# Second attention layer: scores from two fp32r parts, two sides of 64 rows each in the array

## What is computed

```python
q = _apply_rotary((x @ Wq.T).reshape(B, T, H, Dh), cos, sin)
k = _apply_rotary((x @ Wk.T).reshape(B, T, H, Dh), cos, sin)
v = (x @ Wv.T).reshape(B, T, H, Dh)
scores = jnp.einsum('bhqd,bhkd->bhqk', q, k) * scale
scores = jnp.where(causal[None, None], -jnp.inf, scores)
attn = jax.nn.softmax(scores, axis=-1)
out = jnp.einsum('bhqk,bhkd->bhqd', attn, v)
x = x + out.transpose(0, 2, 1, 3).reshape(B, T, C) @ Wo.T
```

## Time and profile before

| | us |
|---|---|
| median of 3 runs | 2464.02 |
| lowest, highest | 2453.02, 2469.33 |
| the profiled execution | 2465.51 |
| its span, first to last instruction | 2463.4 |
| PE busy | 2220.4 |
| DVE busy | 1457.2 |
| ACT busy | 1030.9 |
| POOL busy | 680.1 |

### The profile page before, as it was taken

The page is one execution under the profiler, slowest core; times in us unless marked ns, Lnnn a source line. Parts: engine busy times, 40 slices in busy tenths (PEclk is TensorE's granted clock), DMA queues, the critical chain, the costliest instruction groups (busy, mean ns, idle before and its releaser), DMA issues. The chain is left out here.

```text
span 2463.4 us, 49191 instructions
## 1 busy us (share of the span) xinstructions
PE 2220.4 (90%) x19494; PEld 1810.1 (73%) x19494; DVE 1457.2 (59%) x3308; ACT 1030.9 (42%) x1986; POOL 680.1 (28%) x772
## 2 busy tenths in 40 slices
PE   7799999999999999699879974899999979986998
PEld 7688888888888888577669972455555547776998
DVE  2565564647465554388746644666666627874665
ACT  4333334333333334244335531455555544432554
POOL 3210110101010100165522222433343215652222
PEclk8899999999999999799989986899999999998999
DMA  7300000000000000411547756444444416113775
GB/s 233 117 18 10 10 10 10 10 10 19 2 18 10 10 1 2 130 44 61 206 157 220 235 147 140 79 79 79 80 86 80 74 55 223 48 43 95 233 231 137
DMA packets 155901, 212.68 MB, mean 86 GB/s; under 512 B 51656, under 2 KB 140000, under 8 KB 150368
## 3 DMA queue, kind: packets, MB, share of 16 engines
q1 hardware_dynamic: 142140, 191.38, 27.6%
q0 software_dynamic: 12864, 17.38, 4.3%
q10 hardware_dynamic: 672, 0.79, 0.2%
HBM read 141.80 MB, written 67.69 MB: 85 GB/s over the span
## 5 line engine op out<-in xcount | busy, mean ns | idle before, releaser
L2383 DVE TENSOR_REDUCE b_neg_max<-bank 128x1 f32<-128x512 f32 (+2 forms) x384 | 179.0, 507 | 140.4 <-PE bank L2616 137.9
L2506 ACT ACTIVATE b_probsT<-bank 128x512 f32<-128x512 f32 x320 | 183.1, 603 | 180.2 <-PE bank L2616 155.0
L2113 PE MATMUL bank<-e_hT_hi,k_rwkv 128*128 128x256 f32 x1088 | 214.8, 283 | 2.8 <-DVE e_hT_lo L2016 2.8
L2113 PEld LDWEIGHTS bank<-e_hT_hi,k_rwkv 128*128 128x128 f32 x1088 | 177.0, 191 | 3.6 <-DVE e_hT_lo L2016 3.6
L789 POOL TENSOR_TENSOR probs<-probs,rcp 128x512 f32<-128x512 f32 x64 | 66.9, 1045 | 381.7 <-DVE rcp L658 381.7
L2127 PE MATMUL bank<-v_rwkv_hi,e_hidden_hi 128*128 (+1 forms) x544 | 153.5, 282 | 0.0
L2127 PE MATMUL bank<-v_rwkv_hi,e_hidden_lo 128*128 (+1 forms) x544 | 153.5, 282 | 0.0
L2113 PE MATMUL bank<-e_hT_lo,k_rwkv 128*128 128x256 f32 x544 | 152.3, 280 | 0.0
L2127 PE MATMUL bank<-v_rwkv_lo,e_hidden_hi 128*128 (+1 forms) x544 | 152.1, 280 | 0.0
L2074 ACT ACTIVATE e_relu<-bank,k_bias 128x256 f32<-128x256 f32 x272 | 113.6, 469 | 73.2 <-PE bank L2113 63.1
L2616 PE MATMUL bank<-b_k_stacked,b_q_stacked 96*128 96x512 bf16 (+3 forms) x512 | 126.5, 309 | 0.0
(11 more groups left out here) (364 smaller groups left out, 6252.4 us busy)
## 6 DMA issues: line engine op xcount, KB each, us to landing
k_rwkv<-scratch_k SPq DMA_DIRECT2D x32, 2048.0 KB, 7.3
scratch_b_parts<-b_part SPq DMA_DIRECT2D x96, 128.0 KB, 2.1
b_q_stacked<-scratch_b_parts SPq DMA_DIRECT2D x96, 128.0 KB, 4.4
b_k_stacked<-scratch_b_parts SPq DMA_DIRECT2D x96, 128.0 KB, 4.6
e_rows<-scratch_rows SPq DMA_DIRECT2D x34, 258.0 KB, 7.7
scratch_rows<-f_hq SPq DMA_DIRECT2D x16, 516.0 KB, 8.1
x_tokens<-in_x_dram SPq DMA_DIRECT2D x8, 512.0 KB, 8.0
scratch_x_out<-x_tokens SPq DMA_DIRECT2D x8, 512.0 KB, 2.9
```

The costliest lines, as they stand in the source:

```text
L2113: last = nc.tensor.matmul(data[:, half * ROWS:(half + 1) * ROWS], ff.k_part(i % 2, a)[:, k, at:at + P], hT[b][:, i % 2, k], start=n == 0, ...
L2383: last = nc.vector.tensor_reduce(neg_max[:, half % 2, t, head + e:head + e + 1], data[:, at:at + (t + 1) * P], AX_X, ALU.max, negate=True)
L2506: nc.scalar.activation(probsT[:, ring, u], fl.data("st", pair, u)[:], ACT.Exp, scale=DB ** -0.5).then_inc(fl.released("st", pair, u), 1)
```

## The change

Queries, keys and maxima are split into two fp32r parts instead of three bf16 ones: one cast and one subtraction each. A head has 3 x 16 = 48 rows, 50 with the maxima. Stacks hold the even head of a pair in partitions 0 to 49 and the odd one in 64 to 113. A mask is two matmuls of 64 rows, from an identity and mask of which a second copy has its halves swapped. Where a slot has both kinds of scores, `scores_beside` issues them in turn, one instruction of the turned unit of one head (rows of one half), one of the plain unit of the other head (rows of the other half). The shared unit has both heads, so its two parts are made one after the other with a wait of PE for its own matmuls between them, and it stands third instead of last. Maxima are turned by fp32 matmuls.

```diff
-Q_PARTS, K_PARTS_B = (0, 0, 1, 1, 0, 2), (0, 1, 0, 1, 2, 0)
+Q_PARTS, K_PARTS_B = (0, 0, 1), (0, 1, 0)
+PARTS_B = 2
 STACK = len(Q_PARTS) * DB
-MAX_PARTS = 3
+MAX_PARTS = 2
+ROW_HALF = P // 2
+STACK_DMAS = 2 * 2 * len(Q_PARTS)
 UNITS = (((0, 3, 0),), ((0, 2, P), (0, 0, 0)), ((1, 3, 0),), ((1, 2, P), (1, 0, 0)), ((0, 1, 0), (1, 1, 2 * P)))
+BOTH = len(UNITS) - 1
+TURNED_ORDER, SCORED_ORDER = (0, 1, BOTH, 2, 3), (2, 3, BOTH, 0, 1)
...
-        ident16, masks = buf("ident16", [P, P], BF16), buf("masks16", [P, 2, 2 * P], BF16)
+        ident16, masks = buf("ident16", [P, 2, P], BF16), buf("masks16", [P, 2, 2, P], BF16)
-        parts = [buf(f"b_part{c}", [P, 2, T], BF16) for c in range(3)]
-        stacked = [[buf(f"b_{side}_stacked{b}", [P, HEADS_H, T], BF16) for b in range(STACK_BUFS)] for side in ("q", "k")]
+        parts = [buf(f"b_part{c}", [P, 2, T], F32R) for c in range(PARTS_B)]
+        stacked = [[buf(f"b_{side}_stacked{b}", [P, PAIRS_H, T], F32R) for b in range(STACK_BUFS)] for side in ("q", "k")]
...
-        LOADS, CONSTS, ONES = 7 * 16, 2, 2
-        SPLITS, ROWS = 5, slice(0, MAX_PARTS * HEADS_H)
+        LOADS, CONSTS, ONES = 7 * 16, 3, 2
+        SPLITS, ROWS = 2, slice(0, MAX_PARTS * HEADS_H)
...
+    def stack(side, b, at):
+        for row, c in enumerate((Q_PARTS, K_PARTS_B)[side]):
+            for e in range(2):
+                first = e * ROW_HALF + row * DB
+                sp.dma_start(stacked[side][b][first:first + DB, :, :].bitcast(F32),
+                             parts_out[at, c].rearrange("(j e d) t -> e d j t", e=2, d=DB)[e]).then_inc(stack_loaded[b], 16)
...
-        for c in range(3):
-            sp.dma_start(parts_out[at, c], parts[c][:, at % 2]).then_inc(s["parts_stored"], 16)
+        for c in range(PARTS_B):
+            sp.dma_start(parts_out[at, c], parts[c][:, at % 2].bitcast(F32)).then_inc(s["parts_stored"], 16)
         if half >= STACK_BUFS and side == 0:
-            sp.wait_ge(*full("st", (half - STACK_BUFS + 1) * PAIRS_H - 1, last_unit))
-        sp.wait_ge(s["parts_stored"], (at - 1) * 48)
-        for row, c in enumerate((Q_PARTS, K_PARTS_B)[side]):
-            sp.dma_start(stacked[side][b][row * DB:(row + 1) * DB, :, :],
-                         parts_out[at, c].rearrange("(h d) t -> d h t", d=DB)).then_inc(stack_loaded[b], 16)
+            sp.wait_ge(*full("st", (half - STACK_BUFS + 1) * PAIRS_H - 1, last_turned))
+        sp.wait_ge(s["parts_stored"], (at - 1) * PARTS_B * 16)
+        stack(side, b, at)
...
-        v_.tensor_tensor(rotated[:, 1], rotated[:, 1], parts[0][:, 1], ALU.subtract).then_inc(s["keys_rest"], 1)
-        ready((s["mid_done"], 2))
-        v_.tensor_tensor(parts[2][:, 1], rotated[:, 1], parts[1][:, 1], ALU.subtract).then_inc(s["keys_split"], 1)
+        v_.tensor_tensor(parts[1][:, 1], rotated[:, 1], parts[0][:, 1].bitcast(F32), ALU.subtract).then_inc(s["keys_split"], 1)
...
-        g.tensor_tensor(rotated[:, at % 2], rotated[:, at % 2], parts[0][:, at % 2], ALU.subtract).then_inc(s["rest_done"], 1)
-        ready((s["mid_done"], at + 1))
-        g.tensor_tensor(parts[2][:, at % 2], rotated[:, at % 2], parts[1][:, at % 2], ALU.subtract).then_inc(s["lo_done"], 1)
+        g.tensor_tensor(parts[1][:, at % 2], rotated[:, at % 2], parts[0][:, at % 2].bitcast(F32), ALU.subtract).then_inc(
+            s["lo_done"], 1)
...
         after(g.tensor_copy(out(0), src))
-        after(g.tensor_tensor(rest[:], src, out(0), ALU.subtract))
-        after(g.tensor_copy(out(1), rest[:]))
-        after(g.tensor_tensor(rest[:], rest[:], out(1), ALU.subtract))
-        after(g.tensor_copy(out(2), rest[:]))
+        after(g.tensor_tensor(out(1), src, out(0).bitcast(F32), ALU.subtract))
...
-
-    def middle(n, step):
-        at = n * 4 + step
-        act.wait_ge(*((s["keys_rest"], 1) if (n, step) == FIRST_KEYS else (s["rest_done"], by_pool(at))))
-        nc.scalar.activation(parts[1][:, at % 2], rotated[:, at % 2], ACT.Copy).then_inc(s["mid_done"], 1)
...
-        act.dma_start(stacked[0][b][STACK:STACK + MAX_PARTS, :, :],
-                      max_out[half].rearrange("(c h) t -> c h t", h=HEADS_H)).then_inc(max_loaded[b], 16)
+        for e in range(2):
+            first = e * ROW_HALF + STACK
+            act.dma_start(stacked[0][b][first:first + MAX_PARTS, :, :].bitcast(F32),
+                          max_out[half].rearrange("(c j e) t -> e c j t", e=2, c=MAX_PARTS)[e]).then_inc(max_loaded[b], 16)
...
-    for dst, src in ((ident16[:], core.ident), (masks[:].rearrange("p a n -> p (a n)"), raw_masks)):
-        nc.scalar.activation(dst, src[:], ACT.Copy).then_inc(s["consts_done"], 1)
+    swapped_halves = ident16[:, 1].rearrange("p (h n) -> p h n", h=2)[:, ::-1, :]
+    for dst, src in ((ident16[:, 0], core.ident[:]), (swapped_halves, core.ident[:].rearrange("p (h n) -> p h n", h=2)),
+                     (masks[:].rearrange("p a b n -> p (a b n)"), raw_masks[:])):
+        nc.scalar.activation(dst, src, ACT.Copy).then_inc(s["consts_done"], 1)
...
+    def mask(data, pair, u, turned, e, roll, start):
+        rows = half_rows(e)
+        region, src = data[:].rearrange("p (n k) -> p n k", k=P), masks[rows, int(turned), roll, :]
+        if u == BOTH:
+            region = region[:, 2 * e + (0 if turned else 1), :]
+        elif len(UNITS[u]) == 1:
+            region = region[:, 0 if turned else 3, :]
+        else:
+            region = region[:, 0:2, :] if turned else region[:, 0:4:3, :]
+            src = src.unsqueeze(1).to_broadcast([ROW_HALF, 2, P])
+        nc.tensor.matmul(region, ident16[rows, roll, :], src, start=start, stop=False, skip_group_check=True)
+    def part(data, pair, u, turned, e, n):
+        b, j = half_of(pair) % STACK_BUFS, pair % PAIRS_H
+        rows = half_rows(e, STACK + MAX_PARTS if turned else STACK)
+        q, k = stacked[0][b][rows, j], stacked[1][b][rows, j]
+        t, at = UNITS[u][e if u == BOTH else n][1:]
+        size = (t + 1) * P
+        tile, first = ((TT - 1 - t) * P, (TT - 1 - t) * P) if turned else (t * P, 0)
+        weights, moving = (k, q) if turned else (q, k)
+        return nc.tensor.matmul(data[:, at:at + size], weights[:, tile:tile + P], moving[:, first:first + size], start=False,
+                                stop=True, skip_group_check=True)
+    def alone(one, start):
+        for roll in range(2):
+            mask(*one, roll, start and roll == 0)
+        for n in range(parts_in(one[2])):
+            last = part(*one, n)
+        return last
+    def beside(one, other, start):
+        for roll in range(2):
+            mask(*one, roll, start and roll == 0)
+            mask(*other, roll, start and roll == 0)
+        for n in range(parts_in(one[2])):
+            last = part(*one, n), part(*other, n)
+        return last
+    heads_done = 0
+    def wait_for_heads(*last):
+        nonlocal heads_done
+        for instruction in last:
+            instruction.then_inc(s["head_done"], 1)
+            heads_done += 1
+        pe.wait_ge(s["head_done"], heads_done)
     def scores(pair, u, turned):
         name = ("st" if turned else "s", pair, u)
...
-        if u == last_unit:
-            at = 0 if turned else P
-            region = data[:].rearrange("p (h n) -> p h n", h=2)[:, :, at:at + P]
-            nc.tensor.matmul(region, ident16[:], mask.rearrange("p (h n) -> p h n", h=2), start=True, stop=False,
-                             skip_group_check=True)
-        elif len(UNITS[u]) == 1:
-            at = 0 if turned else 3 * P
-            nc.tensor.matmul(data[:, at:at + P], ident16[:], mask[:, 0:P], start=True, stop=False, skip_group_check=True)
+        one = (begin(*name), pair, u, turned)
+        if u == BOTH:
+            wait_for_heads(alone((*one, 0), True))
+            last = alone((*one, 1), False)
         else:
-            region = data[:, 0:2 * P] if turned else data[:].rearrange("p (h n) -> p h n", h=4)[:, 0:4:3, :]
-            src = mask if turned else mask.rearrange("p (h n) -> p h n", h=2)
-            nc.tensor.matmul(region, ident16[:], src, start=True, stop=False, skip_group_check=True)
-        for e, t, at in UNITS[u]:
-            size = (t + 1) * P
-            q, k = stacked[0][b][rows, head + e], stacked[1][b][rows, head + e]
-            tile, first = ((TT - 1 - t) * P, (TT - 1 - t) * P) if turned else (t * P, 0)
-            weights, moving = (k, q) if turned else (q, k)
-            last = nc.tensor.matmul(data[:, at:at + size], weights[:, tile:tile + P], moving[:, first:first + size], start=False,
-                                    stop=True, skip_group_check=True)
+            last = alone((*one, UNITS[u][0][0]), True)
         last.then_inc(fl.filled(*name), 1)
+    def scores_beside(pair, u, ahead, w):
+        one, other = (begin("st", pair, u), pair, u, True), (begin("s", ahead, w), ahead, w, False)
+        if u == BOTH:
+            wait_for_heads(*beside((*one, 0), (*other, 1), True))
+            last = beside((*one, 1), (*other, 0), False)
```

(26 more changed lines are left out.)

## The result

| | before | after |
|---|---|---|
| median, side by side on one chip (4 runs each) | 2458.52 us | 2516.80 us |
| lowest, highest | 2447.08, 2469.33 | 2504.80, 2519.28 |
| profiled execution | 2465.51 | 2516.46 |
| its span | 2463.4 | 2514.3 |
| plain scores alone (of it at 1.2 GHz) | 44.2 (23.7) | 56.1 (42.4) |

The ratio is 1.0235, 95% interval 1.0199 to 1.0272. The profiled executions differ by 51 us, the medians by 58. The parts are cut at the starts of the first and last score products of each kind, so they differ by some tenths from the earlier trace rows; the differences are +11.9, +34.7, +6.6, -0.6 and -1.6 us, together +51.

What follows compares the result with a forecast made beforehand. PE was taken as the engine to look at, though it and DVE wait in turn. Terms 10 + 8 + 11 + 8 + 2 - 9 - 2 = +28 us on 2464 gave 2492 us, range 2445 to 2548.

Steps and rivals of the forecast that it cites:

- C: Rival, chance 0.12: the two halves' fp32 weight loads go in turn, +0.11 us each pair; 2530 us.
- D: Rival, chance 0.14: fp32r matmuls with 128 moving columns run at plain fp32 rate, 0.21 instead of 0.05 us; 2512 us.
- Matmuls of a pair: Both halves' score matmuls run at once: wide 0.38, narrow 0.43, shared 0.79; 2.41 us a slot instead of 3.10.
- E: Rival, chance 0.07: matmuls of the two halves run in turn, some +1.4 us a slot; 2572 us.
- Change of tile shape: Projections and transposes between scores change PE's tile shape: 26 changes in 8 slots at 0.09 us, +0.29 us a slot.
- What DVE makes of it: At the slot's end DVE's reading holds the third pair's plain bank; net +0.18 us a slot, +10 us, plus +8.
- outside this burst: Outside the three units at the slot's end: shared for wide +0.24, wide for narrow -0.29, shape changes +0.29 us.
- My +8 us for DVE's swap: In half the slots DVE's cosine product and shuffle precede maxima behind the products, losing PE's 0.29 us: +8 us.
- B, no pacing by the banks: Rival, chance 0.22: DVE's reads do not hold the third pair, the slot saves 0.40 us; 2449 us.
- Maxima turned: Turning maxima by plain fp32 instead of bf16 matmuls, in the early place: +0.67 us, 16 times, +11 us.
- Plain scores alone: The part making only plain scores, paced by DVE and projections: bounds 0 and +8, taken as +2 us.
- Stacked keys: Stacks are stored some 3.7 us earlier, taking 9 off PE's 10.8 us of waits for stacked keys.

Runs made afterwards that it cites:

- the third bank: Changed kernel with three PSUM banks for plain scores and two for turned ones, instead of two and three: 2489.21 us, ratio 1.0155.
- the transposes: Changed kernel with maxima turned by PE transposes instead of fp32 matmuls: 2500.47 us, ratio 1.0196.
- idle-row fillers: Changed kernel with two unread 512-column matmuls before each unit, in its idle 64 rows, where plain scores are alone: 2505.75 us, ratio 1.0211.
- the five banks: Changed kernel with transposed maxima, five banks for scores made alone, three plain and two turned where both are: 2467.07 us, ratio 1.0050.
- the kernel with the sides in turn: Changed kernel with turned and plain scores issued one after the other, not instruction by instruction: 2535.70 us, ratio 1.0337.

## Why the prediction was right, and where its sum was short

Direction and range held: 2516.8 lies within 2445 to 2548, above the 2477 to 2508 of my own case. In part that is luck: the range reached so high for rivals C (2530) and D (2512), and neither came. The mechanism was right in kind, the sum too small: it gave +28 us; the profiled executions differ by 51. The middle part was to be 430 to 445 us and took 454.3. Step by step:

- **Matmuls of a pair.** Right in kind: halves and their fp32 loads overlap, and a 128-column fp32r product takes 0.06 us (1823.75 to 1823.81), so C, D and E fall. The shortest pairs were a bit longer than my figures: wide about 0.41 (0.38), narrow 0.47 (0.43), shared 0.83 (0.79), 2.6 us a slot instead of 2.41.
- **Change of tile shape.** Right in its price: from the last projection matmul to the mask 1823.34 - 1823.03 = 0.31 us, where the same matmul in a row takes 0.22. That is 0.09 us a change. But the untouched work grew by 16.8 us, where half of the 26 changes in 8 slots (each block's exit) make 93 x 0.09 = 8.3; the other half falls into the score blocks. The remaining 8.5 us I had nothing for; the projections' longest blocks went from 3.2 to 3.7 us, and PE stood at 1.2 GHz for 23 us more.
- **What DVE makes of it.** The block that I worked out came a little better than forecast, as a difference: 2.28 us for 2.38 before, where I had 1.88 for 1.94 and 0.09 more for its exit (PE also starts 0.14 us after DVE, 1824.80 to 1824.94, and not 0.05). The failed step is "outside this burst": there I priced every unit at PE's own pace. That holds for the pair alone at the products (+0.30 for +0.24) and the one behind them (-0.17 for -0.29 and 0.09 of shape), but not where no early or late work stands between and four plain units in a row meet two banks. For the 16 blocks of four without late work my prices make -0.26 us (-0.06, -0.29, +0.09) and it was +0.28; for the 11 without early work +0.18, and it was +0.53. That is 0.54 x 16 + 0.35 x 11 = 12.5 us, and the third bank took mostly these blocks down. My +8 us for DVE's swap meant the unit behind the products. Of the 26 slots of the middle part with a swap 12 have late work behind that unit, and there it takes 0.50 us with a swap as without. Another 12 are among the 16 blocks of four, and 0.29 x 12 = 3.5 of the 12.5 us were priced by that term; the rest of the 8 did not come.
- **B, no pacing by the banks.** It was to decide by whether PE's waits for DVE stay near 15 us. Those were waits of weight loads, and the sign as I wrote it, loads waiting several times as long, did not come: the profile now puts hardly any wait of loads down to DVE. The matmuls' waits went from 6.2 to 45 us, and one more bank is worth 29 us in the middle part; that rules B out. The Trainium skill ("TensorEngine Tiling (Array Packing)", PSUM Bottleneck) says that tiling speeds up the matmuls and not the reading of their results; these two numbers agree.
- **Maxima turned.** +0.65 us a time for +0.67 predicted, and 9.1 us in the 14 blocks of the middle; the transposes, 0.44 us a time shorter, returned 6.9 us for 16 x 0.44 = 7.
- **Plain scores alone.** The term most off for its size: +2 taken, from bounds of 0 and +8; measured +11.9, outside them. My bounds let PE's pace be that of the clock of before. It fell (42.4 of 56.1 us at 1.2 GHz, 23.7 of 44.2 before). The idle-row fillers took 7.0 us of it back, and the five banks, with the transposes (1.9 us by themselves), 11.5.
- **Turned scores alone.** +6.6 for +8. **Front.** -0.6 for -2.
- **Stacked keys.** Right: PE's 10.8 us of waits in the middle are gone. PE waits a little longer for the queries' maxima instead, 5.1 us for 3.2. Their DMA issues on ACT took far more than the "some 0.1 us" I gave (below); that this is the reason was not tested.

So the 23 us missing in the sum are some 10 in the plain part and some 15 in the middle: about 8 in the score blocks (12.5 from the blocks of four, less what the swap's term and the blocks of three came out better) and 8.5 in the untouched work. How the middle's 34.7 us divide between waits and the lower clock wasn't separated: the third bank removed both (33.7 us at 1.2 GHz became 11.0). The 23 us more at 1.2 GHz can have cost at most about 12 (an estimate: half of them).

## What to carry to other kernels

Two tiles in the array shorten the making of results (0.67 to 0.47 us for a narrow pair of units), not the reading (0.76 us before and after): before changing to them, count for each place of the order how many results in a row fall on how many banks, and give the reader's side one more bank with the change. A stage in which PE already waits must be costed at the clock it will be granted afterwards, not at that of before. And an experiment that moves work should be costed by what its reader gets later, not by what the maker no longer waits.

## What was unexpected of the hardware

**Order between row halves.** In the kernel with the sides in turn, matmuls issued later but for the other 64 rows start within 10 ns of those issued earlier (1822.49 and 1822.50 above), past a queued matmul of the first side, as the kernel's text orders them. The Trainium skill ("TensorE: Matmul & The Clock Gate", Part 3, The mechanism) calls matmuls strictly first in, first out in start and end; this run shows otherwise for tiles of different rows.

**DMA issues on ACT.** One issue of the maxima's return takes ACT 0.24 us before and 0.60 after, with two a half instead of one, so 1.2 us a half for 0.24. Durations (least, median, most) of the issue in the kernel after:

```profile
L2561 ACTq DMA_DIRECT2D b_q_stacked<-scratch_b_max x32: 599/599/1204, 1562.1 to 2033.7; - x32
```

and before:

```profile
L2557 ACTq DMA_DIRECT2D b_q_stacked<-scratch_b_max x16: 237/238/259, 1552.6 to 1984.8; - x16
```

**The clock.** In the part with plain scores alone, where the scores use half of the rows and PE stands idle for 10 us, 8 of them until DVE has its maxima, PE was granted 1.2 GHz for 42.4 of 56.1 us. Matmuls in the idle rows alone, at the same order of work, cut that to 11.6 of 49.1 us.
